# Block 0 of a four-block transformer kernel: two key tiles weighed every second step, narrow matmul operands padded with zeros

## What is computed

```python
for i in range(NL):                                   # NL = 6, H = 16 heads of 8
    xn = _adaln(x, noise_emb, n1_w[i], n1_b[i])
    q, k, v = jnp.split(xn @ qkv_w[i].T, 3, axis=-1)  # q, k rotated by _rope
    x = x + _attn(q, k, v, src_mask) @ so_w[i].T      # 56 keys
    xn = _adaln(x, noise_emb, n2_w[i], n2_b[i])
    q = _rope(xn @ cq_w[i].T); k = _rope(context @ ck_w[i].T); v = context @ cv_w[i].T
    x = x + _attn(q, k, v, ctx_mask) @ co_w[i].T      # 1500 keys
    xn = _adaln(x, noise_emb, n3_w[i], n3_b[i])
    x = x + (gelu(xn @ f1_w[i].T + f1_b[i]) @ f2_w[i].T + f2_b[i])
```

## Time and profile before

| | us |
|---|---|
| median of 3 runs | 6655.85 |
| lowest, highest | 6644.8, 6667.22 |
| span of the profiled execution | 6652.9 |
| block 0's score steps, from about 200 to about 3440 us | some 3240 |
| PE busy over the span | 6159.3 (93%) |
| DVE busy over the span | 3930.9 (59%) |
| ACT busy over the span | 3325.9 (50%) |

### The profile page before, as it was taken

The page is one execution under the profiler, slowest core; times in us unless marked ns, Lnnn a source line. Parts: engine busy times, 40 slices in busy tenths (PEclk is TensorE's granted clock), DMA queues, the critical chain, the costliest instruction groups (busy, mean ns, idle before and its releaser), DMA issues.

```text
span 6652.9 us, 141291 instructions
## 1 busy us (share of the span) xinstructions
PE 6159.3 (93%) x56229; PEld 4429.8 (67%) x56229; DVE 3930.9 (59%) x8713; ACT 3325.9 (50%) x6401; POOL 2242.2 (34%) x2179
## 2 busy tenths in 40 slices
PE   6899899999999989999989999999789999989998
PEld 4566566665666656666653877777567777756983
DVE  3777777777777777777765334444544444444553
ACT  1565656656566565665654334444333333333763
POOL 4554555555555555555520000000011111136440
PEclk6899999999999999999989889999789999998998
DMA  1665656656666565665740010000000000021000
GB/s 56 105 111 83 99 94 99 106 91 103 93 98 111 85 100 100 96 108 87 110 95 5 13 38 29 29 33 24 26 15 15 10 15 12 13 81 36 2 1 23
DMA packets 396488, 407.90 MB, mean 61 GB/s; under 512 B 125575, under 2 KB 372946, under 8 KB 393786
## 3 DMA queue, kind: packets, MB, share of 16 engines
q1 hardware_dynamic: 395834, 398.85, 33.8%
HBM read 158.00 MB, written 0.46 MB: 24 GB/s over the span
## 4 chain that ended last, share of the span: by engine, by line
PE 69%; DVE 8%; POOL 7%; issue 6%; ACT 4%; DMA 2%; SPq 1%; POOLq 1%; DVEq 0%; ACTq 0%
PE psum L2214 10%; PE psum L2181 9%; PE psum L1551 6%; PE psum L1539 6%; PE psum L1525 6%; PE psum L2226 4%; PE psum L1565 4%; PE psum L1573 3%; PE psum L1671 3%; POOL slot_context L3399 2%; PE psum L434 2%; DVE row_max L1890 2%; PE psum L420 2%; PE psum L1680 1%; DMA key_stack<-key_parts 1%
## 5 line engine op out<-in xcount | busy, mean ns | idle before, releaser
L1890 DVE TENSOR_REDUCE row_max<-psum 112x1 f32<-112x500 f32 x2304 | 1443.7, 669 | 285.3 <-PE psum L1539 280.3
L2011 ACT ACTIVATE weights<-psum 125x448 f32<-125x448 f32 x2304 | 1155.4, 544 | 769.3 <-PE psum L1525 754.3
L1525 PEld LDWEIGHTS psum<-query_stack,key_stack 121*125 121x125 bf16 x9216 | 830.4, 140 | 368.4 <-issue 165.5
L1539 PE MATMUL psum<-key_stack,query_stack 97*112 97x500 bf16 x2304 | 907.8, 395 | 102.1 <-DVE row_max L1890 78.9
L1525 PE MATMUL psum<-query_stack,key_stack 121*125 121x112 bf16 x9216 | 932.3, 224 | 70.1 <-ACT weights L2011 65.0
L2767 POOL TENSOR_TENSOR l_ctx_v<-l_ctx_v,l_ctx_w 125x512 f32<-125x512 f32 x48 | 61.1, 1272 | 2223.1 <-DVE l_ctx_v L2761 2223.1
L2294 DVE TENSOR_REDUCE l_stat<-psum 128x1 f32<-128x1500 f32 (+1 forms) x224 | 391.6, 1748 | 576.6 <-PE psum L2181 576.6
L2214 PE MATMUL psum<-l_ctx_v,l_turned 125*128 125x128 f32 x5376 | 713.6, 281 | 16.0 <-ACT l_turned L2252 12.3
L2214 PEld LDWEIGHTS psum<-l_ctx_v,l_turned 125*128 125x128 f32 x5376 | 643.0, 191 | 58.5 <-ACT l_turned L2252 39.9
L1551 PE MATMUL psum<-weights,values 125*17 125x112 f32 x18432 | 678.0, 266 | 0.2 <-ACT weights L2011 0.2
L1551 PEld LDWEIGHTS psum<-weights,values 125*17 125x17 f32 x18432 | 379.4, 97 | 263.6 <-ACT weights L2011 144.7
(11 more groups left out here) (527 smaller groups left out, 10264.3 us busy)
## 6 DMA issues: line engine op xcount, KB each, us to landing
key_stack<-key_parts SPq DMA_DIRECT2D x1728, 125.0 KB, 4.5
ctx_t<-in_ctxT SPq DMA_DIRECT2D x96, 750.0 KB
l_ctx_v<-in_ctxV SPq DMA_DIRECT2D x32, 750.0 KB
query_stack<-query_parts SPq DMA_DIRECT2D x576, 28.0 KB, 3.7
l_ctx_t<-in_ctxT SPq DMA_DIRECT2D x16, 750.0 KB
slot_context<-in_ctxV SPq DMA_DIRECT2D x16, 750.0 KB
key_stack<-ctx_mask_rows SPq DMA_DIRECT2D x576, 3.9 KB
sm_w<-in_sm_w SPq DMA_DIRECT2D x3, 2048.0 KB
```

Source lines behind the costliest of these rows:

```text
L1525: mm = e.matmul(self.k.psum[0:KN, h, (p % 4) * QC:(p % 4 + 1) * QC], ks[:, p, kt * KN:(kt + 1) * KN], q[:, p * QC:(p + 1) * QC])
L1539: e.matmul(self.k.psum[0:QC, 2 + n % 2, 0:500], q[0:ROWS_MAX, p * QC:(p + 1) * QC], ks[0:ROWS_MAX, p, c * 500:(c + 1) * 500]).then_inc(sel ...
L1890: e.tensor_reduce(self.largest[:, i % PAIRS, i // PAIRS:i // PAIRS + 1], k.psum[0:QC, 2 + i % 2, 0:500], AX.X, ALU.max, negate=True).then_ ...
L2011: e.activation(half(self.p[kt % 2], h), self.k.psum[0:KN, h, 0:HALF], ACT.Exp).then_inc(self.exped.sem, 1)
```

## The change

1. `weigh_tensor` runs for two key tiles together, after the scores of every even step (tiles kt-2 and kt-1; the last two of a slot at kt 0 of the next). The ring of `p` has four buffers in place of two, and the exponential waits for the weighing four tiles back.
2. The self weights move out of `phase_tensor` into `self_weigh_tensor`, called directly behind `weigh_tensor` and ahead of `fixed_tensor`. `T_SELF` becomes 27, 31, ... 55 (27, 29, ... in the first phase), so that `a+3` is an even step. The planner lists the self weights first in their step.
3. Operands with few rows or columns get zeros around them: the self weights' operands, the mask row and both flips 96 rows in place of 56, 1 and 56; the rows of the maxima and the self values 72 columns in place of 25 and 56.
4. DVE zeroes the ten padded pieces at the start.

```diff
+WIDE = 72
+TALL = 96
+XN_TAIL = WIDE - S
-T_SELF = lambda ph: [26 + (2 * i if ph < 0 else 9 * i // 2) for i in range(BH)]
+T_SELF = lambda ph: [27 + (2 if ph < 0 else 4) * i for i in range(BH)]
+RING_P = 4
...
-            self.p = [sb(f"weights{i}", [KN, T])[:, :] for i in range(2)]
+            self.p = [sb(f"weights{i}", [KN, T])[:, :] for i in range(RING_P)]
-            self.m_part = sb("neg_max_parts", [QC, 1 + 3 * PAIRS], BF16)[:, :]
+            self.m_part = sb("neg_max_parts", [QC, WIDE], BF16)[:, :]
-            self.spt = [sb(f"self_pt{i}", [S, H * S])[:, :] for i in range(2)]
-            self.sv = sb("self_v", [S, BH, PAIRS, 17])
+            self.spt = [sb(f"self_pt{i}", [TALL, H * S])[:, :] for i in range(2)]
+            self.sv = sb("self_v", [TALL, BH, PAIRS, 17])
...
+                order += self.self_weigh_order(ph, t) + self.fixed_order(s, kt) + self.phase_order(ph, t)
...
-            e.transpose(side.bank(*key)[:, 0:S], self.o, k.ident[0:S, 0:S]).then_inc(side.filled, 1)
+            e.transpose(side.bank(*key)[:, 0:TALL], self.o_tall, k.ident[0:TALL, 0:TALL]).then_inc(side.filled, 1)
...
-            e.transpose(side.bank(*key)[0:1 + 3 * PAIRS, 0:QC // 2].bitcast(BF16), self.m_part,
+            e.transpose(side.bank(*key)[0:WIDE, 0:QC // 2].bitcast(BF16), self.m_part,
...
-                mm = e.matmul(side.bank(*key)[0:S, i * 128:(i + 1) * 128], of_batch(k.xn, c * BH + 4 * g + i),
+                lo = (c * BH + 4 * g + i) * S
+                mm = e.matmul(side.bank(*key)[0:WIDE, i * 128:(i + 1) * 128], k.xn_wide[:, lo:lo + WIDE],
...
-                if 0 <= s < NS and kt > 0:
+                if 0 <= s < NS and kt > 0 and kt % 2 == 0:
+                    self.weigh_tensor(e, s, kt - 2)
                     self.weigh_tensor(e, s, kt - 1)
                 if 1 <= s <= NS and kt == 0:
+                    self.weigh_tensor(e, s - 1, KT - 2)
                     self.weigh_tensor(e, s - 1, KT - 1)
+                self.self_weigh_tensor(e, s // BH, 12 * (s % BH) + kt)
                 self.fixed_tensor(e, s, kt)
                 self.phase_tensor(e, s // BH, 12 * (s % BH) + kt)
...
-                    if h == 0 and s * KT + kt >= 2:
-                        e.wait_ge(self.weighed.sem, self.weighed(s, kt) - 2)
-                    e.activation(half(self.p[kt % 2], h), self.k.psum[0:KN, h, 0:HALF], ACT.Exp).then_inc(
+                    if h == 0 and s * KT + kt >= RING_P:
+                        e.wait_ge(self.weighed.sem, self.weighed(s, kt) - RING_P)
+                    e.activation(half(self.p[kt % RING_P], h), self.k.psum[0:KN, h, 0:HALF], ACT.Exp).then_inc(
```

More of the change, by code:

```diff
@@ L1383, in fixed_order, with self_weigh_order @@
         return order
+    def self_weigh_order(self, ph, t):
+        if NEXT_OF(ph) is None:
+            return []
+        return [("sw", ph, i) for i, a in enumerate(T_SELF(ph)) if t == a + 3]
     def phase_order(self, ph, t):
@@ L1601, in fixed_tensor, with self_weigh_tensor @@
             e.wait_ge(self.parts_ready.sem, self.parts_ready(s + 1))
-            e.transpose(side.bank(*key)[0:1 + 3 * PAIRS, 0:QC // 2].bitcast(BF16), self.m_part,
+            e.transpose(side.bank(*key)[0:WIDE, 0:QC // 2].bitcast(BF16), self.m_part,
                         k.ident_b[0:QC, 0:QC]).then_inc(side.filled, 1)
+    def self_weigh_tensor(self, e, ph, t):
+        side = self.side
+        for _, _, i in self.self_weigh_order(ph, t):
+            key = ("sw", ph, i)
+            for g in range(2):
+                e.wait_ge(side.emptied("st", ph, i, g), side.after("st", ph, i, g))
+            if i % 4 == 0:
+                e.wait_ge(side.emptied("sv", ph, i // 4), side.after("sv", ph, i // 4))
+            e.wait_ge(side.emptied(*key), side.before(*key))
+            for p in range(PAIRS):
+                j, g = p % 4, p // 4
+                mm = e.matmul(side.bank(*key)[32 * j:32 * j + 17, g * QC:(g + 1) * QC], self.sv[:, i, p, :],
+                              self.spt[i % 2][:, p * QC:(p + 1) * QC], start=g == 0, stop=True, skip_group_check=True)
+            mm.then_inc(side.filled, 1)
     def hidden(self, f):
@@ L1682, in phase_tensor @@
                     tr.then_inc(side.filled, 1)
-            if t == a + 3:
-                key = ("sw", ph, i)
-                for g in range(2):
-                    e.wait_ge(side.emptied("st", ph, i, g), side.after("st", ph, i, g))
-                if i % 4 == 0:
-                    e.wait_ge(side.emptied("sv", ph, i // 4), side.after("sv", ph, i // 4))
-                e.wait_ge(side.emptied(*key), side.before(*key))
-                for p in range(PAIRS):
-                    j, g = p % 4, p // 4
-                    mm = e.matmul(side.bank(*key)[32 * j:32 * j + 17, g * QC:(g + 1) * QC], self.sv[:, i, p, :],
-                                  self.spt[i % 2][:, p * QC:(p + 1) * QC], start=g == 0, stop=True, skip_group_check=True)
-                mm.then_inc(side.filled, 1)
             if t == a + 4:
@@ L1706, in phase_tensor @@
                 e.wait_ge(side.emptied(*key), side.before(*key))
-                e.transpose(side.bank(*key)[:, 0:S], self.so, k.ident[0:S, 0:S]).then_inc(side.filled, 1)
+                e.transpose(side.bank(*key)[:, 0:TALL], self.so_tall, k.ident[0:TALL, 0:TALL]).then_inc(side.filled, 1)
             if t == a + 6 and i % 2 == 1:
@@ L1852, in phase_vector @@
                     e.wait_ge(side.filled, side.at("sw", ph, i - 2))
-                e.tensor_copy(self.spt[i % 2][:, BANK:T], side.bank(*key)[0:S, 0:T - BANK]).then_inc(side.emptied(*key), 1)
+                e.tensor_copy(self.spt[i % 2][0:S, BANK:T], side.bank(*key)[0:S, 0:T - BANK]).then_inc(side.emptied(*key), 1)
             if t == a + 4:
@@ L1862, in phase_vector, with clear_vector @@
                 e.tensor_tensor(d, side.bank(*key)[:, 0:QC], d, ALU.add).then_inc(side.emptied(*key), 1)
+    def clear_vector(self, e):
+        for tall in (self.one_row, self.src_mask, self.m_part, self.o_tall, self.so_tall, self.spt[0], self.spt[1],
+                     self.sv[:, :, :, :], self.k.xn_wide[:, T:],
+                     half(self.k.xn_wide, 1)[:, 0:XN_TAIL]):
+            e.memset(tall, 0.0)
+        e.drain().then_inc(self.cleared.sem, 1)
     def vector(self, e):
@@ L1987, in phase_scalar @@
                     e.wait_ge(side.filled, side.at("sw", ph, i - 2))
-                e.activation(self.spt[i % 2][:, 0:BANK], side.bank(*key)[0:S, :], ACT.Copy).then_inc(side.emptied(*key), 1)
+                e.activation(self.spt[i % 2][0:S, 0:BANK], side.bank(*key)[0:S, :], ACT.Copy).then_inc(side.emptied(*key), 1)
             if t == a + 3:
```

34 lines of the change are left out of this document (19 added, 15 removed).

## The result

| | before | after |
| --- | --- | --- |
| median, us (eight runs each) | 6656.5 (6644.8 to 6673.9) | 6691.26 (6678.36 to 6699.59) |
| span of the profiled execution, us | 6652.9 | 6689.6 |

The ratio is 1.0046 with a 95% interval of 1.0034 to 1.0058: the change made the kernel **slower by 0.46%**, 35 us, where I had forecast 17 us less. It lies in my range, on the wrong side of no change. In the two spans the difference is 36.7 us. Up to the first score step the time fell from 200.1 to 193.5 us; from the first score step of block 0 to its last it grew from 3237.0 to 3274.9, and that is the whole of the loss. The rest grew by 5.3, and it moved between 3204 and 3226 us over all kernels of this study, so I read nothing from it. The time up to the first score step moved too, between 185 and 205 us.

A forecast was written before the change was run, and what follows sets the result against it. The prediction took PE as the bound, busy 102.6 of 103.5 us in the self stretch. Eleven phases at -7.3 - 1.7 + 6.4 (-29 us) and the last phase's +12 gave -17 us: 6639 us, range 6540 to 6715.

The forecast's parts named there:

- What a visit costs, and what each entry costs: PE's narrow mode: each merged pair saves 0.21 us, 121 in all; padding some 105; 226 if PE were always last.
- Rival D: Padded operands don't take their neighbours' mode, so the entries stay and 11 x 6.6 us are lost: 6712 us; chance 0.05.
- rival B: PE is the last to arrive nearly everywhere: 6430 us in full, 6543 with half of it; chance 0.20.
- Rival E: PE's sequencer can't deliver two tiles' weights and self weights in a row: +196 us, 6835; chance 0.04.
- The odd steps with little in them: Quiet slots: emptied odd steps wait for DVE's reads of the maximum; 1.45 us slower per slot, 4.3 per phase.
- The stretches with the norms: Steps 9 to 25 and 62 to 71: six of twelve pairs lose 0.35 us each, 2.1 us slower per phase.
- Where the gain counts: Self stretch, steps 27 to 61: less PE work saves 10.4 us per phase, less two new waits, 7.3 us net.
- Rival C: The maximum's two banks also stop the self stretch's pairs, costing 0.40 each: 6699 us with nine, 6760 with all; chance 0.21.
- The rest of the self stretch and step 26: Padding and self weights save 6.6 us in the self stretch; POOL's moved operation saves 1.7 us at step 26, per phase.
- 6684 us in the prediction: Steps 34 and 46: POOL's moved operation could block five small DVE operations, up to 2.07 us each, 46 us over eleven phases.
- Sum: Eleven phases at -7.3 - 1.7 + 6.4 give -29 us, the last phase +12: together -17 us, 6639 us.

The follow-up runs named there:

- e2_single: The changed kernel without the pairs: one key tile weighed every step, as before; 6541.49 us, 0.9823 of before.
- e5: The kernel before with DVE's reads of the maximum cut from 500 to 250 columns; 6598.94 us, 0.992 of before.
- e6: The changed kernel with DVE's reads of the maximum cut from 500 to 250 columns; 6569.13 us, ratio 0.9875.
- e4: The changed kernel with the pairs at odd steps instead of even ones and the self steps moved one back; 6493.52 us, 0.9746 of before.
- e8: The changed kernel with an exponential in place of the square root in block 0's norms, so no table changes there; 6615.6 us, ratio 0.994.
- e14: The changed kernel with one tile weighed every step and an exponential in place of the norms' square root; 6502.0 us, 0.9764 of before.
- e3_mixed: The changed kernel with pairs only in the self stretch (steps 27 to 61), one tile every step elsewhere; 6552.49 us, 0.984 of before.
- e9: e3_mixed with POOL's blocked queries made a step earlier and ACT's copy of the self sums ahead of the value chunk's; 6566.91 us, 0.9862 of before.
- e1_pad: The kernel before with the padded operands and nothing else; 6611.44 us, 0.9923 of before.

## Why the prediction went wrong, step by step

**What a visit costs, and what each entry costs: right.** The second tile's weights were priced at 0.40 us and take 0.383 in step 32; M to W and W to the next matmul moved as worked out. The mask row takes 0.17 instead of 0.27, and behind a self flip S comes after 0.09 us instead of 0.19 and is 0.39 long instead of 0.44 (1126.83 and 1126.92 in phase 3). Rival D (the padding does nothing) is out, and rival B (PE last nearly everywhere) with it: the time rose.

**Rival E (PE's sequencer can't deliver so many in a row) is out.** 32 matmuls of W take 0.96 us at 1262.48 with no gap, and self weights follow 0.076 behind W's last group. The Trainium skill (TensorE: Matmul & The Clock Gate, "Wait — 56ns, not 53.3ns?") gives an issue time of about 62 ns a matmul where hardware decode is off, by which these 32 would take an estimated 2.0 us; the trace does not agree, with 0.96. The longest run of such matmuls in it is these 32 and the self weights' 16.

**The odd steps with little in them: the sum right, its parts in some measure by luck.** 1.45 us per quiet slot were forecast, and a slot of 27.9; measured is 27.82, +4.14 us per phase for the three against +4.3, or +4.50 for the pairs alone (e2_single), and +11.2 us in the last phase against +12. Pair by pair, in steps 84 to 95 against e2_single, (1, 2) and (5, 6) cost 0.38 each (0.40 forecast) and (7, 8) 0.19 (0.25), but (3, 4) and (9, 10) cost 0.16 and 0.18 where I had nothing, and (11, 0) of steps 83 and 84 costs nothing where I had 0.40. e5 and e6 show that DVE's read is in that loop, e4 that the same pairs gain where the pair stands at an odd step. Not in my working were S's wait behind ACT's value copy and the one for the DMA of the key tiles. I worked from M alone: in the three quiet parts of a phase M waits 2.4 us more for DVE than in e2_single, 2.1 more for that DMA, and S 1.7 more for ACT. How much of the time each of them holds isn't separated.

**The stretches with the norms: the sign right, the term mis-sized.** This is the step that failed by most: I took six of twelve pairs at 0.35, 2.1 us, and left the clock out. Measured is 6.4 for the pairs (e2_single). Without table changes it is 4.5 (e8 less e14), which would be twelve pairs at 0.37, but they don't pay alike: (15, 16), (25, 26) and (69, 70) cost 1.64, 1.26 and 1.24 us there, and (13, 14) and (21, 22) gain 0.42 and 0.69. No single wait was isolated in these steps. The other 1.9 come with the tables and the clock behind them, which I had named and then set to nothing.

**"Where the gain counts": the pairs' part of this step failed.** It rests on the sentence that a microsecond less of PE work is a microsecond less of time there. I took 18 pairs at 0.21, 3.8 us, as gained, less 3.1 for the turn's and the transposes' waits: 0.7 us gained. They cost 1.24 (1.87 in e3_mixed). PE does work less (from e2_single to the changed kernel its busy time falls by 2.1 us of the stretch), but its idle time goes from 0.74 to 3.26. I had allowed 0.25 us for one new wait per batch; in step 31 there are two, 0.22 for ACT and 0.38 for POOL, as e9 shows by taking both away (-0.60). In step 37 nothing is gained either (3.647 us with and without the pair): there PE waits for DVE's heads_out (9.5 us in all, against 5.5 in e2_single), which goes through the same three side banks as the turn and the transposes; no run takes this wait away. Rival C had the sign for this stretch, but neither the size (18 pairs at 0.07 to 0.10 us lost, where it has 0.40) nor the cause: it blamed M's two banks, and the waits found are of the side work. A busy PE meant only that the others finished just before it; how much ahead they finished, operation by operation, I read for the turn alone.

**The rest of the self stretch and step 26: right together, not one by one.** Padding, self weights behind W and the new self steps were to give 6.6 us in the self stretch and 1.7 at step 26. In e2_single steps 27 to 61 give 3.96 and steps 9 to 26 give 4.55, 8.5 against 8.3; with the first batch's 1.67 put back where it stood, 5.6 and 2.9. What I had not seen is the move itself: a self stretch of 96 us was out of reach by that alone. Steps 62 to 71 also gave 1.0 us and the quiet parts 0.36 (e2_single), for which I had nothing; of these the padding alone has 0.55 and 0.36 (e1_pad). In the changed kernel the same place reads, against the earlier trace rows:

```profile
1104.00 0.62 DVE L1857 TENSOR_TENSOR l_k<-l_k,ln_square 128x448 f32<-128x448 f32 x1
...
1105.36 0.39 PE L1552 MATMUL psum<-key_stack,query_stack 97*112 97x500 bf16 x1 [1.65 <-DVE row_max L1917]
...
1108.23 1.69 POOL L2129 TENSOR_TENSOR l_qd<-l_q,head_of_feature 128x896 f32<-128x896 f32 x1
```

The rope sum takes 0.62 instead of 1.92, POOL's operation 1.69 instead of 2.07, and M's wait is 0.94 shorter. Steps 26 to 28 together, over which the moved scores cancel, fell from 13.99 to 11.14 us (medians of the steps, added). The block that the Trainium skill's rule (SBUF — State Buffer, "SBUF: two separate sides") would have put on L1739 to L1747 (6684 us in the prediction) did not happen here, since POOL does its key operation first in those steps; it did happen in e9, where the operation was moved beside them. That the changed kernel came out at 6691, near that 6684, has other causes.

**Sum.** Per phase the forecast was -7.3 - 1.7 + 6.4 = -2.6 us; the table has +2.33, 4.9 more. The pairs around the norms are 4.35 of it (6.45 for 2.1), those of the self stretch 1.9 (+1.24 for -0.7), those of the quiet parts 0.2; the rest of the change gave 1.6 more than I had (9.9 for 8.3). Over eleven phases that is 54 us, and the result lies 52 above the forecast (the last phase, the start and the rest come to -2 together in the profiled executions). So the step that turned the sign is the term for the pairs around the norms, 48 us; the one in the self stretch adds 21, and the better rest takes 17 back.

## What to carry to other kernels

When a merger leaves steps without the work that filled them, ask of every wait in those steps how long before PE its releaser was ready; a share of busy time near 99% doesn't answer that, since a releaser that is ready just before PE looks the same there as one that is ready long before it. Merge where another engine's latency covers the longer visit, and keep the work spread where several engines take turns: the same merger lost 150 us in one placement, and with the pairs at odd steps and none from step 24 to 61 the kernel came out 118 us below the version without it. A change of several parts should be run in parts, for here one part gained 115 us and was hidden by the other.

## What the runs showed of the hardware that I had not expected

A DVE operation on eight columns beside a POOL operation grew from 0.17 to 1.60 us, and its bf16 neighbour from 0.18 to 1.02; the length is set by POOL's operation, not by its own. A matmul whose operand has one row takes 0.33 us, and 0.33 when it is padded to 96 rows; it then starts 0.44 instead of 0.53 behind the four fp32 transposes, and the row behind it 0.17 instead of 0.27 behind it. And a wait of PE behind a norm can cost more than its length: behind a wait of 2.16 us M takes 0.64 us instead of 0.38, at the lower clock level, and over block 0 the pairs brought 103 us more at that level than e2_single has.
